# A message-passing layer on one core: the first edge of equal source nodes is found by a weight column in the merging matmul

## What is computed

```python
w = relu(edge_feature @ W_fc1) @ W_fc2
w0, w1, w2, w3, w4 = split(w, [64, 128, 160, 192], axis=-1)
xs, xv = s[dst], v[dst]
out0a = w0 * xs
out0b = w3 * (einsum('emi,ei->em', xv, sh1) * INV_SQRT3)
out1a = (w1 * xs)[:, :, None] * sh1[:, None, :]
out1b = w2[:, :, None] * xv
out1c = w4[:, :, None] * (cross(xv, sh1[:, None, :]) * INV_SQRT2)
agg = segment_sum(concatenate([out0a, out0b, out1a, out1b, out1c]), src, num_segments=N) / DENOM
```

## Time and profile before

| what | value |
|---|---|
| device time, median of 3 runs | 1383.28 us |
| device time of the profiled execution | 1387.66 us |
| its span, first to last instruction | 1385.8 us |
| POOL busy | 1066.5 us, 77% |
| PE busy | 919.5 us, 66% |
| DVE busy | 880.1 us, 64% |
| ACT busy | 428.5 us, 31% |
| granted TensorE clock, mean | 0.783 of full speed |

### The profile page before, as it was taken

How to read it: one execution, slowest core, us unless ns; L and a number is a source line. 1 busy time by engine, 2 the same in 40 slices (tenths; PEclk the granted TensorE clock), 3 DMA queues, 4 the chain that set the end, 5 groups by cost and what they waited for, 6 DMA issues and landing times.

```text
span 1385.8 us, 26047 instructions
## 1 busy us (share of the span) xinstructions
PE 919.5 (66%) x5648; PEld 780.3 (56%) x5648; DVE 880.1 (64%) x3693; ACT 428.5 (31%) x839; POOL 1066.5 (77%) x830
## 2 busy tenths in 40 slices
PE   7498766757757768577677675776766757769103
PEld 5387655646646657466566574665655646658102
DVE  7899747657566576575675766656647667579105
ACT  5154332322323323223233232232332323325101
POOL 1777788888888888888878888788788887887880
PEclk9699877786877877778778787787787877779556
DMA  9635555555454555554555555545554555456557
GB/s 351 165 92 102 105 80 86 99 80 105 81 80 105 78 84 101 80 105 80 80 105 80 88 97 81 104 79 82 105 78 88 97 80 106 79 78 90 52 55 274
DMA packets 124075, 139.89 MB, mean 101 GB/s; under 512 B 34241, under 2 KB 99585, under 8 KB 123970
## 3 DMA queue, kind: packets, MB, share of 16 engines
q0 software_dynamic: 79296, 74.04, 38.2%
q1 hardware_dynamic: 44674, 64.92, 15.1%
HBM read 86.24 MB, written 52.66 MB: 100 GB/s over the span
## 4 chain that ended last, share of the span: by engine, by line
DMA 31%; POOL 26%; DVE 23%; issue 14%; PE 3%; DVEq 2%; ACT 0%; POOLq 0%; SPq 0%; ACTq 0%
DMA sums<-to_add,add_idx 15%; DMA sums<-spare,add_idx 15%; POOL turn_space L388 9%; POOL sums L406 8%; DVE products_space L805 6%; POOL rows L388 5%; POOL spare L388 5%; DVE products_space L834 4%; DVE before L873 2%; DVE same L872 2%; DVE products_space L832 2%; DVE products_space L831 2%; DVE radial L847 1%; DVE msg L858 1%; DVE turn_space L816 1%
## 5 line engine op out<-in xcount | busy, mean ns | idle before, releaser
L507 PE MATMUL t_ps<-w,products_space 128*128 128x128 f32 (+1 forms) x1248 | 225.2, 312 | 350.6 <-DVE products_space L834 350.6
L523 PEld LDWEIGHTS o_ps<-w,pT 128*128 128x128 f32 (+1 forms) x2496 | 360.5, 223 | 40.7 <-issue 37.9
L406 POOL DMA_INDIRECT sums<-to_add,add_idx x208 | 326.6, 1570 | 67.9 <-issue 47.3
L507 PEld LDWEIGHTS t_ps<-w,products_space 128*128 128x128 f32 (+1 forms) x1248 | 166.3, 160 | 373.7 <-issue 335.8
L523 PE MATMUL o_ps<-w,pT 128*128 128x96 f32 (+1 forms) x2496 | 376.6, 309 | 0.0
L406 POOL DMA_INDIRECT sums<-spare,add_idx x208 | 326.6, 1570 | 64.4 <-issue 46.0
L631 ACT ACTIVATE pT<-t_ps 128x512 f32<-128x512 f32 (+1 forms) x312 | 185.4, 594 | 320.2 <-PE t_ps L507 319.7
L897 DVE TENSOR_TENSOR add_idx<-key,from_col 128x4 int32<-128x4 f32 x104 | 16.9, 163 | 371.0 <-DMA sums<-spare,add_idx 206.7
L388 POOL DMA_INDIRECT turn_space<-node_table,to_idx x186 | 187.1, 1006 | 56.7 <-issue 46.7
L640 ACT ACTIVATE msg<-o_ps 128x448 f32<-128x448 f32 x208 | 113.0, 543 | 335.8 <-PE o_ps L523 327.4
L538 PE MATMUL d_ps<-msg,same 128*128 128x192 f32 x832 | 197.0, 365 | 28.4 <-ACT spare L652 20.6
(11 more groups left out here) (96 smaller groups left out, 865.6 us busy)
## 6 DMA issues: line engine op xcount, KB each, us to landing
from_row<-nodes_row SPq DMA_DIRECT2D x52, 512.0 KB
ef<-edge_t SPq DMA_DIRECT2D x52, 256.0 KB
turn_space<-node_table SPq DMA_DIRECT2D x768, 0.6 KB
spare<-node_table SPq DMA_DIRECT2D x768, 0.6 KB
turn_space<-sums SPq DMA_DIRECT2D x9, 480.0 KB, 7.0
sums<-zeros SPq DMA_DIRECT2D x6, 672.0 KB, 9.2
sums<-to_add,add_idx POOLq DMA_INDIRECT x208, 3.6
sums<-spare,add_idx POOLq DMA_INDIRECT x208, 3.6
```

Source lines behind the costliest of these rows:

```text
L406: pool.indirect_dma_start(sums[t], bass.IndirectOffsetOnAxis(ap=add_idx[:, 2 * v + h, j:j + 1], axis=0), to_add[2 * v + h][:, j, :], None, ...
L507: ins = nc.tensor.transpose(t_ps[(3 * u + c) % 2][0:ROWS[c], j * P:(j + 1) * P], prod[:, u % 2, j, a:e], ident)
L523: ins = nc.tensor.matmul(o_ps[m][:, base + oc:base + oc + n], pT[c][u % 2][:, cols], w[0:ROWS[c], wc:wc + n], start=(q == 0 and c == 0), s ...
```

## The change

The masked comparison of line 873 and its mask are gone. A column of 3^(63-p), p being the edge's place in its tile, stands ahead of the messages (`ranked`), so that `merge` sums it over the edges of equal node along with the rest; a column for partition p that holds no earlier edge sums to at most 2 * 3^(63-p). DVE compares the merged column with that limit in `repeats`, and `rows_to_add` derives the row number. Since the column is there only after merge and collect, these two steps run for group g-4 in step g, not for g-2, and the first two groups, whose numbers were made ahead of the loop, are no exception any more. A row of `to_add` grows from 192 to 208 numbers, of which 193 are written and 192 scattered. DVE's own wait for the landed scatters falls away (the wait for `sums_ready` implies it), and SP's `load_from` waits for `same_ready`.

```diff
+SUM_AT = 16
+SUM_ROW = SUM_AT + M
-        msg = sb("msg", [P, 2, J, OUTS])
+        ranked = sb("ranked", [P, 2, J, 1 + OUTS])
+        msg = ranked[:, :, :, 1:1 + OUTS]
-        before = sb("before", [P, J, P])
-        key = sb("key", [P, 3, 2, J])
-        to_add_0 = sb("to_add_0", [P, UNROLL, J, M])
+        key = sb("key", [P, 2, UNROLL, J])
+        to_add_0 = sb("to_add_0", [P, UNROLL, J, SUM_ROW])
...
                 if valid(b - 2, BLOCKS):
-                    sp.wait_ge(idx_ready, 2 * b - 2)
+                    sp.wait_ge(same_ready, 2 * b - 2)
...
-                            to_add[2 * v + h][:, j, :], None, compute_op=ALU.add,
+                            to_add[2 * v + h][:, j, SUM_AT:SUM_ROW], None, compute_op=ALU.add,
...
-                    ins = nc.tensor.matmul(d_ps[:, q * M:(q + 1) * M], same[:, u % 2, 2 * m + q, :],
-                                           msg[:, u % 2, 2 * m + q, 0:M], start=(q == 0), stop=(q == 1),
+                    ins = nc.tensor.matmul(d_ps[:, q * (1 + M):(q + 1) * (1 + M)], same[:, u % 2, 2 * m + q, :],
+                                           ranked[:, u % 2, 2 * m + q, 0:1 + M], start=(q == 0), stop=(q == 1),
...
-                nc.scalar.activation(to_add[u][:, 2 * m:2 * m + 2, :],
-                                     d_ps[:, 0:2 * M].rearrange("p (q o) -> p q o", q=2),
+                nc.scalar.activation(to_add[u][:, 2 * m:2 * m + 2, SUM_AT - 1:SUM_ROW],
+                                     d_ps[:, 0:2 * (1 + M)].rearrange("p (q o) -> p q o", q=2),
...
+                nc.vector.tensor_scalar(ranked[:, :, :, 0], w[:, W_RANK:W_RANK + 1].unsqueeze(2).broadcast_to([P, 2, J]),
+                                        1.0, None, ALU.mult)
...
                 if valid(g - 2, GROUPS):
                     dve.wait_ge(summed, 2 * g - 2)
-                    dve.wait_ge(idx_ready, g - 1)
+                if valid(g - UNROLL, GROUPS):
+                    dve.wait_ge(repeats_ready, g - UNROLL + 1)
                 for j in range(J):
-                    nc.vector.tensor_scalar(same[:, k, j, :], row, col, None, ALU.is_equal)
-                    nc.vector.scalar_tensor_tensor(before[:, j, :], row, col, lower, ALU.is_equal, ALU.mult,
-                                                   accum_out=key[:, 0, k, j:j + 1])
+                    nc.vector.tensor_scalar(same[:, k, j, :], from_row[:, par, (h * J + j) * P:(h * J + j + 1) * P],
+                                            from_col[:, par, h * J + j:h * J + j + 1], None, ALU.is_equal)
...
-                dve.wait_ge(same_ready, g + 1)
-                nc.vector.scalar_tensor_tensor(key[:, 2, k, :], key[:, 0, k, :], 0.5, key[:, 1, k, :],
-                                               ALU.is_gt, ALU.mult).then_inc(repeats_ready, 1)
+                dve.wait_ge(sums_ready, 2 * g + 2)
+                nc.vector.scalar_tensor_tensor(key[:, 1, u % UNROLL, :], to_add[u][:, :, SUM_AT - 1],
+                                               w[:, W_FIRST:W_FIRST + 1], key[:, 0, u % UNROLL, :],
+                                               ALU.is_le, ALU.mult).then_inc(repeats_ready, 1)
...
                 dve.wait_ge(repeats_ready, g + 1)
-                if valid(g - RING, GROUPS):
-                    for j in range(J - TABLES, J):
-                        t, n = landed(b - LOOP, u, j)
-                        dve.wait_ge(added[t], n)
-                nc.vector.tensor_tensor(add_idx[:, u, :], key[:, 2, k, :], from_col[:, par, h * J:(h + 1) * J],
-                                        ALU.add).then_inc(idx_ready, 1)
+                nc.vector.tensor_scalar(add_idx[:, u, :], key[:, 1, u % UNROLL, :], -1.0, w[:, W_DUMP:W_DUMP + 1],
+                                        ALU.mult, ALU.add).then_inc(idx_ready, 1)
...
                 vectors(g - 2, u2, 0)
-                early = isinstance(g, int) and g - 2 < EARLY_GROUPS
-                if not early:
+                if not (isinstance(g, int) and g - 2 < EARLY_GROUPS):
                     same_nodes(g - 2, u2, 2 * i + (u - 2) // RING)
+                repeats(g - 4, u4)
                 radial_part(g - 2, u2, 1)
-                if not early:
-                    repeats(g - 2, u2)
+                rows_to_add(g - 4, u4)
                 vectors(g - 2, u2, 1)
-                if not early:
-                    rows_to_add(g - 2, u2, 2 * LOOP * i + (u - 2) // 2)
```

37 lines of the change are left out of this document (15 added, 22 removed).

## The result

The changed kernel takes 1404.13 us (median of four runs, 1401.85 to 1405.14) against 1383.58 us for the kernel before (four runs, 1383.23 to 1386.11): a ratio of 1.0138 [1.0123, 1.0153]. It is 20.5 us slower, where 1382.0 was forecast, with 1375 to 1389 as the range. The profiled execution took 1403.12 us, its span is 1401.3: 15.5 us above the span before.

The account below looks back on a forecast made before the run. The prediction took POOL, issuing transfers without a pause, to bound the kernel. All terms were 0 except -1.3 us for fewer disturbed gathers: 1383.3 - 1.3 = 1382.0 us, range 1375 to 1389.

Parts of the forecast that it names:

- What bounds the kernel: POOL issues its transfers without a pause, 1315.5 us of the 1385.8 us span; DVE's waits are back-pressure.
- DVE is the bound: Rival: DVE's removed 112 us would all come off the time, giving 1271 us; chance 0.02.
- Removed comparisons, new key instructions: DVE loses 112 us, all into idle time; key instructions run beside gathers: 0. Hits by the comparisons themselves: -1.3 us.
- The waits: DVE's wait at line 897 goes; its 370.6 us of waiting mostly move to line 847, behind ACT: 0.
- `load_from` waits for an earlier event; its loads came in time already: 0: On SP, the loads of node numbers are released by an earlier event, at no cost: 0.
- so some change of the landing is free: POOL's scatters: landing takes 3.6 us, a table is used again after 5.6 us; no cost from moderately later landing.
- Numbers two steps later: Row numbers reach POOL two DVE steps later; cover holds at the start, in mid-run and at the end: 0.
- 193 columns, 386 in the copy, 832 bytes a row: Wider merge and copy cost 1.7 and 2.6 ns on waiting engines; row step costs scatters 0, bounds ±2 us.
- Hits: Two-operand DVE instructions lengthen gathers that start beside them; of 20 us, ±5 us may change, without direction.
- scatters keep 1.57 us: Sign of being right: POOL's mean scatter time stays the same; another mean would show the forecast wrong.
- More hits: Rival: DVE lines 805 or 815 meet one more gather in each block, +7 to +11 us, 1390 to 1394; chance 0.17.
- The rival of 1405: Row numbers come late, or the new `tensor_scalar` blocks POOL's descriptor writing, 23 us, giving 1405 us; chance 0.02.

Follow-up runs that it names:

- e1: The changed kernel with DVE again waiting at the end of each step for the landed scatters of the group eight back: 1386.29 us, ratio 0.9998.
- e2: The changed kernel with SP's load of node numbers held until the sixth scatter of block b-6 has landed: 1393.13 us, ratio 1.0036.
- e16: e2 with one added 160-column sum of one SBUF operand in each DVE step, some 0.3 us, behind its wait for ACT: 1434.48 us, ratio 1.0359.
- e17: e13 with one added 160-column sum of one SBUF operand, some 0.3 us, in each DVE step: 1426.55 us, ratio 1.0304.
- e11: e1 with three unread DVE additions of two 384-column SBUF operands added to each step: 1451.77 us, ratio 1.0223.
- e12: e1 with three unread DVE sums over 384 columns of one SBUF operand added to each step: 1442.73 us, ratio 1.0135.
- e3: The kernel before with 16 row-number buffers instead of 8, so DVE need not wait for landed scatters: 1418.03 us, ratio 1.0240.
- e4: The kernel before with SP's load of node numbers held until a block's first scatter has landed, so loads fall among scatters: 1446.74 us, ratio 1.0427.
- e13: e2 with DVE held once a block until the first scatter of the group eight back has landed: 1387.64 us, ratio 1.0006.
- e5: The kernel before with only SP's row-by-row fetches waiting for a block's first scatter to land: 1412.26 us, ratio 0.9969.
- e9: The same kernel as e13, in an earlier round where the kernel before varied more: 1423.42 us, ratio 1.0035.

## Why the forecast was wrong

**What bounds the kernel: right.** POOL issues from first gather to last scatter before and after, and 105 us less DVE work moved nothing (e1: 0.9998). The rival "DVE is the bound" (1271) is out.

**Removed comparisons, new key instructions: right.** DVE's busy time fell by 105.5 us for the 112 forecast, all of it hidden. The -1.3 us for hits that the comparisons themselves had made is of the right size: in the kernel before, gathers that began while line 873 ran lost 2.7 us. But other lines took the place, and the sum of the gathers is unchanged.

**The waits: right in where they went, wrong in "0".** They moved to line 851 as said. The failed step is "DVE's wait at line 897 goes ... 0". I asked whether anything comes late when the wait goes, and nothing does. I did not ask what it kept in phase. DVE went on when a group's scatters had landed, and so did all that follows DVE.

**"`load_from` waits for an earlier event; its loads came in time already: 0": the step that cost most.** It asks only whether the data come early enough, not what the transfer collides with. The step next to it says that a table is used again after 5.6 us and that a landing takes 3.6, "so some change of the landing is free". It has 2 us of slack by that; with a burst of 768 KB beside it the landing of 685.28 took 2.9 us longer, and POOL stood 1.1 us. The row was there: of the five long gaps before, the longest (133.52, 2.55 us) follows a `from_row` load that SP had issued at 125.83. With 19 bursts issued after a block's scatters have begun, for 3 before, 17 of them followed by a long gap, the term that stood at 0 is +9.7 us in the profiled pair; moving the loads in e2 takes 9.9 us off the stretch.

**Numbers two steps later: right.** Group 0's numbers are made at 79.92 us, its first scatter begins at 118.55; the last numbers at 1310.58, the last group's first scatter at 1360.09. Cover is 38.6 and 49.5 us.

**193 columns, 386 in the copy, 832 bytes a row: right.** e1 has them all. The shortest scatter is still 1.55 us.

**Hits: the mechanism was right, place and size were not.** I took ±5 us and looked at gathers only, with "scatters keep 1.57 us" as a sign of being right. The gathers hardly changed (-0.2 us), and the scatters took +6.8 us. DVE's idle time is ended by landings, and landings lie among scatters; this was in my own sentence on the waits, and I didn't carry it over. What an exchange of phases can do was undersized too: e16 and e17 show over 40 us from 0.3 us.

**The rivals.** "More hits" named the slower side, and gave 1390 to 1394. The hits alone are what e2 has, 1.0036 times 1383.28 or 1388.3, which my range would have held. The rest, 1.0% by the ratios, comes from a mechanism that none of the rivals had. (The 25 blocks in that rival are 25 x 0.17 = 4.25, so +2.95 and not +2.8; nothing hangs on it.) The rival of 1405 came near the measured time by accident: `rows_to_add` as a `tensor_scalar` does not block POOL. It stands in e1 as well, at 0.9998, and the 18 transfers that began while it ran (line 895) lost 0.4 us together. The Trainium skill (page "SBUF — State Buffer", section "Who interferes with whom") says that a DVE instruction with two inputs in SBUF contends with a GpSimd instruction that reads SBUF, and, of DVE's modes that use two ports, that whichever engine issues first has the shared ports for its whole instruction. That the two-operand form is the one that hurts agrees with e11 and e12, 336.4 us for 329.7. That `tensor_tensor` cannot shut out POOL's descriptor writing, which the prediction took from the same place and the page itself marks as inferred, does not agree with these runs: POOL's transfers do take longer beside it. The scatter of 738.36, held through several multiplies, goes beyond what the page states.

**What stays open.** Which of the transfers delays the landing. Why a transfer is held for the rest of one DVE multiply in one kernel (before, 743.24) and to the end of all five in another (e17), and once not at all at 0.04 us behind its start. And 5 of the 20.5 us, which the profiled pair doesn't have; the profiled execution of the kernel before, 1387.66, stands among the 15 of e1's round, whose median is 1386.37 and not 1383.58.

## What to carry to other kernels

An engine that is off the bound is still the clock of everything it releases: when a change takes a wait away, ask what it kept in phase, and list for each transfer behind it beside what it ran and beside what it will run. Where a plain load runs beside an accumulating scatter that something waits for, put the load beside work that has slack by an explicit wait (e2: one wait, 10 to 14 us); here a slack of 2 us in a landing did not cover a burst of 768 KB. In a loop whose engines are all let go by the same landings, a collision need not average out: here it came in nearly every block (e3: a gap behind each of 43 loads in the fifth scatter; e17: 41 of 52 seventh scatters held) or in hardly any. A forecast for it needs the phase, or a range as wide as the block count times the longest hit.

## What the runs showed of the hardware

- A scatter lands 3.6 us after its start in the median, and up to 6.7 us (changed) and 7.0 (e4) when SP has issued 768 KB of plain loads about then. (The very last scatter, beside the loading of the tables, took 7.8 us in the kernel before.) The Trainium skill (page "DMA: Bandwidth & Descriptors", section "Latency and other measured facts") gives 2 us of memory latency under high load for 0.2 on the average; the trace shows 3 more for a whole scatter, and cannot say whether that is latency or queueing.
- DVE instructions with two SBUF operands lengthen an indirect transfer that POOL starts while they run: three more a step cost 16 us in sum over those with one operand (e11 against e12). The hold was 0.10 us behind one multiply of line 862, and 1.04 us through the five of line 812. It ended about 0.12 us before the end of that multiply, or of the last of the five (41 of 41 in e17).
- A shift of DVE by 0.3 us changed a kernel of 1390 us by 41 to 45 us, with POOL's gaps nearly unchanged (253.9 us in e16 for 253.4 in e2, 252.5 in e17 for 254.5 in e13).
- In the two rounds in which the kernel before took 1407.65 to 1437.94 us (e5 to e12), a gap of 20 to 34 us stood ahead of POOL's first scatter: in e9 that scatter began at 146.63 us, after a wait of 30.57 us for `add_idx`, in e13, the same kernel, at 119.70. I have not found out why.
